# Cross-attention kernel: softmax sums as columns, and work moved between VectorE, ScalarE, GpSimd and TensorE

## The reference

```
q, k, v = LN(x) @ Wq, ctx @ Wk, ctx @ Wv        # heads of width 64
s = scale * q @ k.T  (+ bias[256, 4096] in the second)
p = softmax(s)                                   # over 4096 context tokens
x = x + concat(p @ v) @ Wo  (+ b_out in the first)
```

## Time and profile before

| what | us |
|---|---|
| median of 3 runs (2177.58 to 2181.44) | 2179.23 |
| the profiled execution | 2181.46 |
| its span, first to last instruction | 2179.7 |
| TensorE busy in the span (88%) | 1920.6 |
| VectorE busy (75%) | 1632.9 |
| GpSimd busy (44%) | 956.5 |
| ScalarE busy (38%) | 838.5 |
| plain cross-attention, about | 0 to 590 |
| biased cross-attention, about | 910 to 2041 |

### The profile page before, as it was taken

The page is one execution under the profiler, slowest core; times in us unless marked ns, Lnnn a source line. Parts: engine busy times, 40 slices in busy tenths (PEclk is TensorE's granted clock), DMA queues, the critical chain, the costliest instruction groups (busy, mean ns, idle before and its releaser), DMA issues. The chain is left out here.

```text
span 2179.7 us, 34477 instructions
## 1 busy us (share of the span) xinstructions
PE 1920.6 (88%) x12512; PEld 1311.0 (60%) x12514; DVE 1632.9 (75%) x2131; ACT 838.5 (38%) x1108; POOL 956.5 (44%) x450
## 2 busy tenths in 40 slices
PE   8999999999458889899999999999999999996226
PEld 5666666666238778666666666666666666664124
DVE  3666666668387356689988999889998889987562
ACT  3655665556230135233343333433343333434001
POOL 0454665546550034024655546555465545646200
PEclk9999999999669589999999999999999999998557
DMA  2000100000100062000000000110000000000001
GB/s 104 8 13 12 58 31 12 12 8 6 40 3 1 1 242 77 10 8 8 5 12 12 12 5 7 54 47 12 0 12 12 12 12 0 12 8 5 20 0 49
DMA packets 27717, 52.45 MB, mean 24 GB/s; under 512 B 4227, under 2 KB 15252, under 8 KB 27156
## 3 DMA queue, kind: packets, MB, share of 16 engines
q1 hardware_dynamic: 27200, 51.60, 7.3%
q10 hardware_dynamic: 468, 0.16, 0.0%
HBM read 51.23 MB, written 0.52 MB: 24 GB/s over the span
## 5 line engine op out<-in xcount | busy, mean ns | idle before, releaser
L297 POOL TENSOR_TENSOR biased_sums<-biased_sums,biased_scores 128x1024 f32<-128x1024 f32 x224 | 529.2, 2363 | 210.0 <-ACT biased_scores L510 205.9
L559 DVE TENSOR_TENSOR biased_scores<-ps,bias 128x1024 f32<-128x1024 f32 x256 | 311.0, 1215 | 79.4 <-PE ps L365 79.4
L510 ACT ACTIVATE biased_scores<-biased_scores 128x1024 f32<-128x1024 f32 x256 | 268.2, 1053 | 245.0 <-DVE biased_scores L580 244.0
L573 DVE TENSOR_TENSOR ps<-ps,biased_scores 128x512 f32<-128x512 f32 x480 | 331.6, 691 | 3.6
L580 DVE TENSOR_TENSOR biased_scores<-biased_scores,ps 128x1024 f32<-128x1024 f32 x256 | 304.9, 1210 | 11.9 <-PE ps L399 11.9
L297 POOL TENSOR_TENSOR plain_sums<-plain_sums,plain_scores 128x1024 f32<-128x1024 f32 x112 | 264.6, 2362 | 84.5 <-ACT plain_scores L510 74.7
L325 PEld LDWEIGHTS ps<-weights_again,context_again 128*128 128x128 f32 x2048 | 238.2, 191 | 70.2 <-issue 33.5
L325 PE MATMUL ps<-weights_again,context_again 128*128 128x128 f32 x2048 | 262.4, 281 | 13.1 <-ACT biased_keys L483 11.0
L316 PE MATMUL ps<-context_again,weights_again 128*128 128x512 f32 x512 | 251.3, 613 | 19.5 <-ACT biased_values L494 16.9
L365 PE MATMUL ps<-biased_queries,biased_keys 64*128 64x256 f32 x2048 | 257.3, 390 | 6.6 <-DVE biased_scores L559 5.8
L573 DVE TENSOR_TENSOR ps<-ps,plain_scores 128x512 f32<-128x512 f32 x240 | 167.3, 697 | 115.7 <-ACT plain_scores L505 111.4
(11 more groups left out here) (356 smaller groups left out, 2304.1 us busy)
## 6 DMA issues: line engine op xcount, KB each, us to landing
context<-in_ctx_t SPq DMA_DIRECT2D x8, 1024.0 KB, 5.4
moe_w<-in_moe_w SPq DMA_DIRECT2D x32, 256.0 KB, 2.8
context_again<-in_ctx_t SPq DMA_DIRECT2D x8, 1024.0 KB, 6.6
weights_again<-in_wqkv SPq DMA_DIRECT2D x45, 128.0 KB, 2.1
bias<-in_fside SPq DMA_DIRECT2D x1, 4096.0 KB, 22.6
biased_w_out<-in_w_out SPq DMA_DIRECT2D x16, 256.0 KB, 2.6
weights<-in_wqkv SPq DMA_DIRECT2D x21, 128.0 KB, 2.1
plain_w_out<-in_w_out SPq DMA_DIRECT2D x8, 256.0 KB, 2.7
```

What stands on the lines that cost most here:

```text
L297: pool.tensor_tensor(both(SUM[:, :, :, :]), both((E[:, 0] if kp == 1 else SUM)[:, :, :, :]), both(E[:, kp, :, :, :]), ALU.add).then_inc(su ...
L510: act.activation(at, at, ACT.Exp).then_inc(exp_done, 1)
L559: dve.tensor_tensor(E[:, kp, :, :, :].rearrange("p (h t) n j -> p h t (n j)", h=2), scores_bank(kp).rearrange("p (h t n) -> p h t n", h=2, ...
L573: ins = dve.tensor_tensor(to, highest, E[:, kp, :, n, :], ALU.max)
```

## The change

- The sums are turned to columns: `turn_sums` makes, per quarter, FOLD as stationary operand times one column of ones (four matmuls of one column instead of one of 512). `shares` becomes a reciprocal of 128x4, behind the peak steps on VectorE.
- `output` is a plain copy by ScalarE (at the end of slot 7). `project` leaves its two heads in two banks, and ScalarE's `take_shares` copies them into Y with the shares as scale: four activations of 128x256, placed behind exponentials 0 and 1 and ahead of the copy of K6.
- The add to x is done by GpSimd, in two additions of 128x512 (one per head).
- Five of the sixteen subtractions, kp = 5, 7, 9, 11, 13, go to GpSimd, which reads the spread peaks from a copy in SBUF (`LOWERS`, one more copy on VectorE between subtractions 1 and 2).
- In the last pair of each stage GpSimd adds up blocks 0 to 7 only; blocks 8 to 15 are added up by TensorE, eight matmuls of one column per block, in the bank of the sums, each two behind the weighing of their slot.
- The banks of queries and projection change places; the sweep `START` is written out ahead of the loop.

The diff, cut to its core:

```diff
+    LAST_SUMS = 8
+    BY_POOL = (5, 7, 9, 11, 13)
...
-        SUMS_SPREAD, TURNED_PEAKS, PROJECTED, QUERIES = 0, 1, 2, 3
+        SUMS, TURNED_PEAKS, QUERIES, PROJECTED, FIRST_QUERIES = 0, 1, 1, 2, 3
...
+                def lower(m, kp):
+                    pool.wait_ge(lower_kept, m + 1)
+                    pool.wait_ge(scores_kept, NP * m + kp + 1)
+                    at = E[:, kp, :, :, :]
+                    pool.tensor_tensor(at, at, LOWERS[:, :, :].unsqueeze(2).to_broadcast([P, HQ, 2, P]),
+                                       ALU.add).then_inc(lowered_too, 1)
+                def add(m, b):
+                    tokens = c.X[:, 2 * b:2 * b + 2, :]
+                    for h in range(2):
+                        pool.wait_ge(shared, 4 * m + 2 * h + 2)
+                        if h == 1:
+                            pool.wait_ge(x_added, 2 * m + 1)
+                        pool.tensor_tensor(tokens, Y[:, h, :, :], tokens, ALU.add).then_inc(x_added, 1)
+                def sweep(m, b, attending, scoring):
+                    for g in range(NG):
+                        if attending and 2 * g + AHEAD + 3 in BY_POOL:
+                            lower(m, 2 * g + AHEAD + 3)
+                        if attending and 2 * g + AHEAD < (NP if scoring else LAST_SUMS):
+                            add_up(m, 2 * g + AHEAD)
+                            add_up(m, 2 * g + AHEAD + 1)
+                    if attending:
+                        fold(m, (NP if scoring else LAST_SUMS) - 1)
...
+                        add(m, b)
+                    if scoring:
+                        add_up(m + 1, 1)
+                        lower(m + 1, AHEAD + 1)
+                        add_up(m + 1, 2)
+                        add_up(m + 1, 3)
...
-                        pe.wait_ge(x_added, p - 1)
+                        pe.wait_ge(shared, 4 * (p - 1))
...
-                    pe.matmul(c.ps[:, SUMS_SPREAD, :], c.ones[:, :], FOLD[:, :, :].rearrange("p a n -> p (a n)"),
-                              start=True, stop=True).then_inc(sums_spread, 1)
+                    for n in range(HQ):
+                        last = pe.matmul(c.ps[:, SUMS, n:n + 1], FOLD[:, n, :], c.ones[:, 0:1],
+                                         start=scoring, stop=True, skip_group_check=True)
+                def add_up(m, kp):
+                    pe.wait_ge(exp_done, NP * m + kp + 1)
+                    for a in range(HQ):
+                        for n in range(2):
+                            pe.matmul(c.ps[:, SUMS, a:a + 1], E[:, kp, a, n, :], c.ones[:, 0:1],
+                                      start=(kp == LAST_SUMS and a == 0 and n == 0), stop=False, skip_group_check=True)
...
                         if attending:
                             weigh(m, g)
+                        if not scoring and 2 * g >= LAST_SUMS:
+                            add_up(m, 2 * g)
+                            add_up(m, 2 * g + 1)
...
+                def output(m):
+                    act.wait_ge(weighed, m + 1)
+                    act.activation(OT[:, :], c.ps[:, OUT, :], ACT.Copy).then_inc(o_kept, 1)
+                def take_shares(m):
+                    act.wait_ge(shares_done, m + 1)
+                    act.wait_ge(projected, m + 1)
...
+                    for h in range(2):
+                        for qt in range(2):
+                            act.activation(Y[:, h, qt, :], c.ps[:, PROJECTED + h, qt * D:(qt + 1) * D], ACT.Copy,
+                                           scale=SHARE[:, 2 * h + qt:2 * h + qt + 1]).then_inc(shared, 1)
...
                         exponential(m + 1, 0)
+                        exponential(m + 1, 1)
+                    elif attending:
+                        output(m)
+                    if attending:
+                        take_shares(m)
+                    if scoring:
                         piece_out(m, ("K", 6))
-                        exponential(m + 1, 1)
...
-                    dve.wait_ge(sums_spread, m + 1)
-                    dve.reciprocal(SHARE[:, :], c.ps[:, SUMS_SPREAD, :]).then_inc(shares_done, 1)
+                    dve.wait_ge(sums_turned, m + 1)
...
+                    dve.reciprocal(SHARE[:, :], c.ps[:, SUMS, 0:HQ]).then_inc(shares_done, 1)
...
-                    if attending:
-                        shares(m)
                     if scoring:
                         find_peaks(m + 1)
                         place_peaks(m + 1)
                     if attending:
-                        output(m)
+                        shares(m)
                     if scoring:
                         for kp in range(AHEAD):
                             lower(m + 1, kp)
-                    if attending:
-                        add(m)
+                            if kp == 1:
+                                dve.tensor_copy(LOWERS[:, :, :].rearrange("p a j -> p (a j)"),
+                                                c.ps[:, LOWER, :]).then_inc(lower_kept, 1)
```

More of the change, by code:

```diff
@@ L175, in cross_attention @@
     AHEAD = 4
+    LAST_SUMS = 8
+    BY_POOL = (5, 7, 9, 11, 13)
+    BY_DVE = [kp for kp in range(NP) if kp not in BY_POOL]
     V_PIECES = [piece for piece in PIECES if piece[0] == "V"]
@@ L195, in cross_attention @@
         DIAG = sb("peaks_diagonal", [P, HQ, P])
-        SHARE = sb("shares", [P, HQ * P])
+        LOWERS = sb("lower_by", [P, HQ, P])
+        SHARE = sb("shares", [P, HQ])
         OT = sb("heads_out", [P, HQ * P])
+        Y = sb("projected_shares", [P, 2, 2, D])
         bo = sb("b_out", [1, D])
@@ L291, in _, with fold @@
             def _(pool):
[L292 to L299, removed]
+                def add_up(m, kp):
+                    pool.wait_ge(exp_done, NP * m + kp + 1)
+                    if kp > 1:
+                        pool.wait_ge(summed, NP * m + kp - 1)
+                    pool.tensor_tensor(both(SUM[:, :, :, :]), both((E[:, 0] if kp == 1 else SUM)[:, :, :, :]),
+                                       both(E[:, kp, :, :, :]), ALU.add).then_inc(summed, 1)
+                def fold(m, count):
+                    pool.wait_ge(summed, NP * m + count)
                     if not (isinstance(m, int) and m == START):
@@ L308, in _ @@
+                if b_out is not None:
+                    pool.wait_ge(b_added, T)
+                sweep(START - 1, 0, False, True)
+                sweep(START, 0, True, True)
+                with pool.Fori(START + 1, START + PAIRS) as m:
+                    sweep(m, 0, True, True)
+                with pool.Fori(START + PAIRS, END - 1) as m:
+                    sweep(m, 1, True, True)
+                sweep(END - 1, 1, True, False)
             @block.tensor
@@ L338, in piece, with queries @@
                         keys(m + 2, g, PIECE)
-                def queries(p):
+                def queries(p, bank=QUERIES):
                     pe.wait_ge(*loaded(p, wq_in))
                     for i in range(DC):
-                        last = pe.matmul(c.ps[:, QUERIES, 0:S], W[:, 0, i, :], c.XNT[:, i, bass.ds(row(p) * S, S)],
+                        last = pe.matmul(c.ps[:, bank, 0:S], W[:, 0, i, :], c.XNT[:, i, bass.ds(row(p) * S, S)],
                                          start=(i == 0), stop=(i == DC - 1))
@@ L406, in project @@
                         for h in range(2):
-                            last = pe.matmul(c.ps[:, PROJECTED, qt * D:(qt + 1) * D],
+                            last = pe.matmul(c.ps[:, PROJECTED + h, qt * D:(qt + 1) * D],
                                              OT[:, h * S + qt * P:h * S + (qt + 1) * P], WO[:, h, :],
-                                             start=(h == 0), stop=(h == 1))
+                                             start=True, stop=True)
                     last.then_inc(projected, 1)
@@ L461, in _ @@
                 pe.wait_ge(c.ln_ready, k + 1)
-                queries(START)
+                queries(START, FIRST_QUERIES)
                 for g in range(2, NG):
@@ L473, in _ @@
                 sweep(START - 1, False, True, True)
-                with pe.Fori(START, END - 2) as m:
+                sweep(START, True, True, True)
+                with pe.Fori(START + 1, END - 2) as m:
                     sweep(m, True, True, True)
@@ L519, in sweep @@
                                 scores_out(m + 1, 2 * g + 1, attending)
+                            if g == NG - 1 and attending:
+                                output(m)
                             piece_out(m, AFTER_SCORES[g])
@@ L547, in _ @@
                 sweep(START - 1, False, True, True)
-                with act.Fori(START, END - 2) as m:
+                sweep(START, True, True, True)
+                with act.Fori(START + 1, END - 2) as m:
                     sweep(m, True, True, True)
@@ L583, in shares @@
                 def shares(m):
-                    dve.wait_ge(sums_spread, m + 1)
-                    dve.reciprocal(SHARE[:, :], c.ps[:, SUMS_SPREAD, :]).then_inc(shares_done, 1)
```

(7 more changed lines are left out.)

34 lines of the change are left out of this document (23 added, 11 removed).

## The result

The changed kernel takes 2223.49 us (median of 4 runs, 2219.3 to 2226.07) against 2179.18 for the kernel before: a ratio of 1.0201, 95% interval 1.018 to 1.0221: slower, clear of noise, while the interval leaves open whether by more or less than 2%. The profiled execution took 2226.07, its span is 2223.2 against 2179.7. Forecast were 2219, range 2190 to 2237, slower with 0.88.

The account below looks back on a forecast made before the run. TensorE was taken to bound the steady pair, and GpSimd's fold to hold up the last pairs; 1.1 + 6.1 + 5.8 - 3.6 + 30 = +39 on 2181.46 gave 2221, or 2219 on the median's footing, range 2190 to 2237.

Parts of the forecast that it names:

- 1.2 for K7: Steady pairs: TensorE's key piece K7 stands still 1.0 to 1.4 for the K6 copy behind the share copies, 20 times.
- The waits given back: Steady pairs: TensorE's waits of 0.21 and 0.73 (biased) and 0.18 before L399 (both stages) go.
- The sums as columns: Each pair: eight one-column records on TensorE take 0.93 against 1.02 for the removed spread, costed at nothing.
- Fold forecast at 58.1: Steady pairs: GpSimd's longer queue ends its fold at 58.1, TensorE wants it at 62.8, so nothing is paid.
- rival (d): GpSimd: a subtraction with a repeated operand costs clearly more, 3.5 say, eating steady pairs' slack: 2250. Chance 0.06.
- the terms +5.8 and -3.6: Last-but-one sweeps: GpSimd's chain puts the next L399 at 63.2, against 57.4 before in plain, 66.8 in biased.
- The working at half clock: Last pairs: TensorE weighs at 3.4 and adds up at 7.0 per group, ending at 77, +22.
- rival (a): Last pairs: TensorE's clock is high there, total +13, 2193. Chance 0.13.
- Rival (b): Last pairs: narrow matmuls cost 0.107 at either clock, bound by loading 128 columns; pair 62, total 2203. Chance 0.12.
- Rival (c): Last pairs, TensorE: one-column matmuls cost almost nothing, loaded under the weighing; -8 each stage, 2173. Chance 0.06.
- the term of 30: Last pairs: most trains at half clock, a part not, so 70 each, +15 in each stage.

Follow-up runs that it names:

- run 1: Changed kernel with ScalarE copying K6 and the queries out first and applying the shares behind them: 2205.28 us.
- run 6: Changed kernel with all sixteen subtractions of every pair back on VectorE (BY_POOL empty): 2200.18 us.
- run 7: Changed kernel with shares behind the K6 copy, the last pair's subtractions on VectorE and wide (512-column) sums there: 2142.32 us, 0.9834 of the kernel before.
- run 8: As run 7, with VectorE making the subtractions of the last two pairs: 2131.89 us, 0.9791 of the kernel before.
- run 3: Changed kernel with the adding up of blocks 8 to 15 left out of the last pair: 2173.54 us.
- run 4: Changed kernel with the last pair's subtractions all on VectorE, TensorE's one-column sums kept: median 2185.25 us.
- run 5: Changed kernel with TensorE's last-pair sums as 512 moving columns, ones stationary, VectorE picking the columns out: 2192.43 us.
- run 10: As run 8, but last-but-one subtractions on VectorE in the plain stage only, and GpSimd adding up ten last-pair blocks: 2124.46 us, 0.9747 of the kernel before.

## Why the prediction was right

**The steady pairs.** Taken was 1.2 for K7, within 1.0 to 1.4; it is 1.17, and run 1 removes it with its edit. The waits given back were as named, and run 6 brings 0.21 and 0.74 back. The sums as columns cost 0.95 against 1.02, as costed. The plain pairs were forecast at +1.02 each and came to +0.91, the biased ones at +0.08 and came to -0.17. Part of the difference lies ahead of L456, which ran into its place without a wait: from K5 to it 1.82 against 2.16, where only 0.18 had been counted. The rest was not traced.

**GpSimd's queue.** Fold forecast at 58.1, measured 57.6; a subtraction with a repeated operand takes 2.36, so rival (d) is out. No steady pair waits for it.

**The last-but-one sweeps.** Both were forecast at 63.2 and took 63.9 and 63.8; the terms +5.8 and -3.6 came to +6.5 and -3.0. In the plain stage the mechanism is the forecast one, GpSimd's chain, by the wait of 2.09 and by runs 6 to 8. In the biased stage the number is right and the mechanism isn't: there VectorE sets the end, as the rows above show, and giving it the five subtractions back made the sweep longer in runs 6 and 8 (65.7, and 66.7 against 64.7). The two chains happen to end close together, so this term came out by luck.

**The last pairs.** The working at half clock gave 77 and the plain stage took 77.3; 70 was taken as a mean of trains at both clocks, and the biased stage took 71.6. So rival (a), a high clock, is out. Rival (b) had a narrow record at the same price at either clock; here 32 records took 6.99 at half clock, 0.22 each, and 3.73 at full clock in run 6, 0.12 each, so it is out too. The rule in the Trainium skill, "TensorE: Matmul & The Clock Gate", section "LDWEIGHTS (loading the stationary operand)", gives a weight load as its columns over 1.2 GHz, with no term for the granted clock; for 128 columns that makes an estimate of 0.107. The trace agrees with it at full clock, where the loads of such a train follow each other every 0.11, and not at half clock, where it is every 0.21. Rival (c), nearly free columns, is out by the same rows, and run 3 shows the whole 28 and 24 come off when they are left out.

**The sum.** The step that was mis-sized is the clock's share in the last pairs: the term of 30 for both stages is 38.9, since the plain stage had no train at a high clock and the biased one only two. The forecast of 39 came near the measured 43.5 because other parts went the other way: the steady pairs cost 3.0 and not 7.2, and 1.9 less lies outside the change (+1.7, +0.1 and -3.7). That the biased stage came so close to 70 is chance in the same sense: where the clock rises or falls in such a pair differs between executions (the plain last pair took 59.9 in run 4 and 55.1 in run 6).

**The cause of the low clock.** The forecast gave two: gaps bring it down, and trains of narrow matmuls do not raise it. Runs 4 and 6 show that narrow trains bring it down without any gap, and runs 5 and 7 that wide ones keep it up, behind a gap and without one. What it is in a narrow train that does it, no run here tells.

## What to carry to other kernels

Work given to TensorE to relieve another engine is to be priced at the clock that this very work leaves: here matmuls of one column kept it busy and for the most part at 1.2 GHz, while the same sums as matmuls of 512 columns ran at 2.4 GHz and took half the time (3.70 against 6.99 for two blocks). When an engine helps in a loop, look at the sweeps where the loop runs short, since its queue is as long there and nothing covers it. And a new step on an idle engine still delays what stands behind it: put it behind the copy that frees the only buffer.

## What the runs showed of the hardware

A TensorE without an idle moment can lose its high clock: in run 4 it went from 1.00 to 0.50 inside a train of 32 one-column records that it had entered at full speed, and stayed there through 31.00 us of full occupation, a third of which were matmuls of 256 columns. In the plain stage of run 6 the same happened one train later. With the same sums as 512-column matmuls the clock rose during the first train and stood at 1.00 through the 19.20 us behind it (run 5).

The clock also goes with how far the executions of one kernel lie apart: ten of run 4 lay between 2178.33 and 2197.63, the slower ones at the lower mean clock, while five of run 10, with wide sums, lay within 4.5.

A GpSimd operation of 128x1024 takes 2.36 as a subtraction with a repeated operand, as the additions do.
